# RK4 stage: VectorE writes the linear values to PSUM, the cubic weights move ahead in its order, fp32 fillers on TensorE

## The chip, the cores and the metric

The kernel runs on one core of one Trainium2 chip. The metric is the device time of the launch in microseconds (us); less is better. Three runs of the kernel before gave a median of 904.41 us.

## The reference

Four residual stages follow each other on x of shape 64 x 32 x 256: a conditioned transformer block, a GRU over time, an attention over blocks, and last the stage of this change, an RK4 integration over the 32 time steps. Cut to that stage:

```python
def _derivative(q, p, drive, coupling, bias):
    i_couple = jnp.tanh(q) @ coupling.T
    dq = q - q ** 3 / 3.0 - p + drive + i_couple + bias
    dp = EPSILON * (q + ALPHA - BETA * p)
    return (dq, dp)
# per time step: four evaluations, each from the result of the one before
dq1, dp1 = _derivative(q, p, ...)
dq2, dp2 = _derivative(q + 0.5 * DT * dq1, p + 0.5 * DT * dp1, ...)
dq3, dp3 = _derivative(q + 0.5 * DT * dq2, p + 0.5 * DT * dp2, ...)
dq4, dp4 = _derivative(q + DT * dq3, p + DT * dp3, ...)
q, p = clip(q + DT / 6 * (dq1 + 2 dq2 + 2 dq3 + dq4)), clip(p + ...)
...
x = x + q_trace      # q of every time step
```

## The kernel before, in words

The state q of a time step is kept as 128 features x 2 chunks x 64 batch entries in fp32. Each chunk ("a" and "b") is a tile of 128 x 64. The four evaluations of a step form one serial ring through three engines:

- ScalarE (ACT) takes the tanh of q by chunks (`th1a`, `th1b` to `th4b`, L1150), and the square of the whole of q (`sq1` to `sq4`, L1153), which it writes to PSUM. It also makes `V3`, `V4`, `V5` as multiples of the clipped state P (L1127) and the drives D of a later step (L1123).
- TensorE (PE; its weight loads are PEld) adds up evaluation k in a pair of PSUM banks, one for each output chunk: first `linear(k, Z)`, two products of the 128 x 128 identity with a linear value (L783), then `coupled`, four products of the coupling matrix with the tanh. The first coupled product of an output chunk streams its 64 columns twice (128 columns, L779), the last streams 64 (L778). Each fp32 matmul stands in the trace as two records. In evaluations 1 and 3 (`chunks_together`) both output chunks take tanh a first and then tanh b; in 2 and 4 (`chunks_in_turn`) the first output chunk is finished before the second is begun.
- VectorE (DVE) computes the next q from the sum in PSUM and a weight w: q2a and q2b (L1693, L1694), q3a and q3b (L1707, L1708), q4a and q4b (L1720, L1721), and qa and qb of the next step (L1736, L1737). The weight is the cubic part, made from the square and q: w1 (L1690), w2 (L1704), w3 (L1717), w4 (L1729). The linear values are E1 (L1733) for evaluation 1 and Z2, Z3, Z4 (L1685, L1702, L1713) for the others. U2, t3, s1 to s4 and P (L1683 to L1727) are parts of these and of the sum for p; L1678 clips q.
- GpSimd (POOL) adds q to the output row and makes U3, U4, m and b4.

The order of the work on each engine is the order in the code, and the tuples `RK_ACT`, `RK_DVE` and `RK_POOL` list it, because each instruction raises its engine's semaphore by one and others wait for the count. DVE's list of a step ends with q4b, s4, P, w4, E1, qa, qb. ScalarE's loop body of a step begins with V5 (made from the P of the step before), then th1a, th1b, sq1, V4; and the body before ends with th4a, th4b, sq4 and V3, which waits for P. Thus V3 and V5 stand ahead of th1a in ScalarE's queue. `mine(...)` is DVE's wait for its own earlier instruction, `coupling(k, c)` its wait for the sum of output chunk c, `act_done` its wait for ScalarE.

Of the kernel before, what the change touches and what calls it, by code (L numbers as in the profile page):

```python
# [8 lines left out]
ALU = mybir.AluOpType  # L9
AX = mybir.AxisListType  # L10

P = 128
B, T, D = 64, 32, 256
KC = D // P
# [13 lines left out]
DT, EPSILON, ALPHA, BETA, CLAMP = 0.01, 0.08, 0.7, 0.8, 20.0  # L28
# [5 lines left out]
C_ = DT / 2  # L34
A_ = EPSILON * C_
SHIFT = ALPHA / BETA
# [15 lines left out]
for _name, _n in (("ada_b", 12), ("qkv_b", 48), ("out_b", 2), ("ffn_b1", 8), ("ffn_b2", 2), ("b_ih", 6),  # L52
# [19 lines left out]
GI_STEPS = (4, 9, 13, 18, 22, 27, 31, 36)  # L72
RK_ACT = ("V5", "th1a", "th1b", "sq1", "V4", "th2a", "th2b", "sq2", "th3a", "th3b", "sq3", "Da", "Db", "th4a", "th4b",
          "sq4", "V3")
RK_DVE = ("q", "U2", "Z2", "w1", "q2a", "q2b",
          "t3", "s1", "Z3", "w2", "q3a", "q3b",
          "s2", "Z4", "s3", "w3", "q4a", "q4b",
          "s4", "P", "w4", "E1", "qa", "qb")
RK_POOL = ("store", "U4", "m", "b4", "U3")
POOL_DVE = ("score_vec", "wo_sum", "wqr", "wo_mean", "wo_c", "copy7", "scaled06", "resid06", "score06", "max06", "scaled7", "resid7", "score7",  # L80
            "score_max", "score_sub",
# [10 lines left out]
def at(step, events, name):  # L92

    return step * len(events) + events.index(name) + 1
# [7 lines left out]
def build(nc, xT, cond, ada_w, qkv_w, out_w, ffn_w1, ffn_w2, w_ih, w_hh, wk, wo, coup, vecs, out):  # L102
# [20 lines left out]
    with ctx:  # L123
# [60 lines left out]
        rk = {}  # L184
# [174 lines left out]
        def _(pe):  # L359
# [247 lines left out]
            def keep_warm(n, bank=TB):  # L607

                for _ in range(n):
                    pe.matmul(ps[:, bank, 0:P], idle[:, :], idle[:, :], start=True, stop=True)  # L610
# [160 lines left out]
            def twice(ap):  # L771

                return ap.unsqueeze(1).to_broadcast([P, 2, B])

            def coupled(k, c, kk, first, last):
                th, w = rk[f"th{k % 2}"][:, kk, :], cpc[:, kk, c * P:c * P + P]
                if last:
                    return pe.matmul(ps[:, RK_BANK[k % 2][c], 0:B], w, th, start=first, stop=last)  # L778
                return pe.matmul(ps[:, RK_BANK[k % 2][c], 0:2 * B], w, twice(th), start=first, stop=last)  # L779

            def linear(k, z):
                for c in range(KC):
                    pe.matmul(ps[:, RK_BANK[k % 2][c], 0:2 * B], ident[:, :], twice(rk[z][:, c, :]), start=True, stop=False)  # L783

            def tanh_done(t, k, half):
                pe.wait_ge(rk_act, RK_ACT_START + at(t, RK_ACT, f"th{k}{half}"))

            def chunks_in_turn(t, k):
                tanh_done(t, k, "a")
                coupled(k, 0, 0, False, False)  # L790
                tanh_done(t, k, "b")
                coupled(k, 0, 1, False, True).then_inc(rk_pe, 1)
                coupled(k, 1, 0, False, False)
                coupled(k, 1, 1, False, True).then_inc(rk_pe, 1)

            def chunks_together(t, k):
                tanh_done(t, k, "a")
                coupled(k, 0, 0, False, False)
                coupled(k, 1, 0, False, False)
                tanh_done(t, k, "b")  # L800
                coupled(k, 0, 1, False, True).then_inc(rk_pe, 1)
                coupled(k, 1, 1, False, True).then_inc(rk_pe, 1)

            keys7_mm()
            blocks_out(0, 0)
# [16 lines left out]
            def first_evaluation():  # L822
                pe.wait_ge(rk_dve, RK_START)
                for c in range(KC):
                    pe.matmul(ps[:, RK_BANK[1][c], 0:B], ident[:, :], rk["E1"][:, c, :], start=False, stop=True).then_inc(rk_pe, 1)

            for t in range(T):
                if t:
                    pe.wait_ge(rk_dve, RK_START + at(t - 1, RK_DVE, "E1"))
                    linear(1, "E1")  # L830
                    chunks_together(t, 1)
                else:
                    first_evaluation()
                pe.wait_ge(rk_dve, RK_START + at(t, RK_DVE, "Z2"))
                linear(2, "Z2")
                if t == 0:
                    keep_warm(WARM_START)
                chunks_in_turn(t, 2)
                pe.wait_ge(rk_dve, RK_START + at(t, RK_DVE, "Z3"))
                linear(3, "Z3")  # L840
                chunks_together(t, 3)
                pe.wait_ge(rk_dve, RK_START + at(t, RK_DVE, "Z4"))
                linear(4, "Z4")
                chunks_in_turn(t, 4)


        @block.scalar
# [331 lines left out]
        def _(dve):  # L1179
# [473 lines left out]
            dve.wait_ge(rk_dve, RK_START - 1)  # L1653
            dve.wait_ge(rk_act, 2)
            dve.tensor_tensor(r_["E1"], r_["D0"], r_["P"], Su).then_inc(rk_dve, 1)
            for t in range(T):
                def mine(name, step=t):
                    dve.wait_ge(rk_dve, RK_START + at(step, RK_DVE, name))

                def pool(name, step=t):  # L1660
                    dve.wait_ge(rk_pool, rk_pool_count(step, name))

                def act_done(name):
                    dve.wait_ge(rk_act, RK_ACT_START + at(t, RK_ACT, name))

                def coupling(k, c):
                    dve.wait_ge(rk_pe, 8 * t + 2 * (k - 1) + c + 1)
                    return ps[:, RK_BANK[k % 2][c], 0:B]

                def half(name, c):  # L1670
                    return rk[name][:, c, :]

                def inc(r):
                    r.then_inc(rk_dve, 1)

                if t:
                    mine("qb", t - 1)
                    inc(dve.tensor_scalar(r_["q"], r_["qraw"], CLAMP, -CLAMP, ALU.min, ALU.max))  # L1678
                else:
                    inc(dve.tensor_copy(r_["q"], r_["qraw"]))  # L1680
                if t == 0:
                    dve.wait_ge(p_dev, 5)
                inc(STT(r_["U2"], r_["P"], -K2, r_[f"D{t % 3}"], M, Ad))  # L1683
                mine("U2")
                inc(STT(r_["Z2"], r_["q"], 1 - A_ * C_, r_["U2"], M, Ad))  # L1685
                if t:
                    act_done("sq1")
                else:
                    dve.wait_ge(rk_first, 1 + RK_FIRST.index("sq1"))
                inc(STT(r_["w"], r_["qsq" if t else "w4"], -(C_ + 1), r_["q"], Ad, M))  # L1690
                a1 = coupling(1, 0)
                mine("w1")
                inc(dve.tensor_tensor(half("q2", 0), a1, half("w", 0), Su))  # L1693
                inc(dve.tensor_tensor(half("q2", 1), coupling(1, 1), half("w", 1), Su))  # L1694

                pool("U3", t - 1)
                inc(STT(r_["t3"], r_["q"], 0.5, r_["U3"], M, Ad))
                if t == 0:
                    dve.wait_ge(rk_first, 1 + RK_FIRST.index("V5"))
                inc(STT(r_["s1"], r_["q"], W1, r_["V5"], M, Ad))  # L1700
                mine("t3")
                inc(STT(r_["Z3"], r_["q2"], -A_ * C_, r_["t3"], M, Ad))  # L1702
                act_done("sq2")
                inc(STT(r_["w"], r_["qsq"], -C_, r_["q2"], Ad, M))  # L1704
                a2 = coupling(2, 0)
                mine("w2")
                inc(dve.tensor_tensor(half("q3", 0), a2, half("w", 0), Su))  # L1707
                inc(dve.tensor_tensor(half("q3", 1), coupling(2, 1), half("w", 1), Su))  # L1708

                pool("b4")  # L1710
                inc(STT(r_["s2"], r_["q2"], W2, r_["s1"], M, Ad))
                mine("q3b")
                inc(STT(r_["Z4"], r_["q3"], 2 * (1 - A_ * C_), r_["b4"], M, Ad))  # L1713
                mine("s2")
                inc(STT(r_["s3"], r_["q3"], W3, r_["s2"], M, Ad))
                act_done("sq3")
                inc(STT(r_["w"], r_["qsq"], -2 * C_, r_["q3"], Ad, M))  # L1717
                a3 = coupling(3, 0)
                mine("w3")
                inc(STT(half("q4", 0), a3, 2.0, half("w", 0), M, Su))  # L1720
                inc(STT(half("q4", 1), coupling(3, 1), 2.0, half("w", 1), M, Su))  # L1721

                mine("q4b")
                if t < T - 1:
                    inc(STT(r_["s4"], r_["q4"], W4, r_["s3"], M, Ad))
                    mine("s4")
                    inc(dve.tensor_scalar(r_["P"], r_["s4"], C_ * (CLAMP - SHIFT), C_ * (-CLAMP - SHIFT), ALU.min, ALU.max))  # L1727
                act_done("sq4")
                inc(STT(r_["w4"], r_["qsq"], -(C_ + 1) / 3, r_["q4"], Ad, M))  # L1729
                if t == T - 1:  # L1730
                    break
                mine("P")
                inc(dve.tensor_tensor(r_["E1"], r_[f"D{(t + 1) % 3}"], r_["P"], Su))  # L1733
                a4 = coupling(4, 0)
                mine("w4")
                inc(STT(half("qraw", 0), a4, 1 / 3, half("w4", 0), M, Su))  # L1736
                inc(STT(half("qraw", 1), coupling(4, 1), 1 / 3, half("w4", 1), M, Su))  # L1737

            ended = RK_START + at(T - 1, RK_DVE, "q4b")
# [322 lines left out]
```

## Time and profile before

| | |
|---|---|
| median of 3 runs | 904.41 us (902.95 to 905.20) |
| profiled execution | 902.81 us, span 900.8 us |
| TensorE, weight loads | 99%, 85% of the span |
| DVE, ACT, POOL | 66%, 46%, 33% |
| mean granted clock of TensorE | 0.998 of full speed |

The span runs from the first to the last instruction of the profiled execution. Timelines give start and duration in us, then engine, line, operation, output and inputs; equal instructions that follow each other are merged with their count. A bracket at the end is the engine's idle time before it and what released it.

### The profile page before, as it was taken

The numbers are of one execution on the slowest core, as the hardware profiler recorded it, in microseconds if no ns is written. First come the engines' busy times: TensorE is split into PE (matmuls) and PEld (weight loads), VectorE is DVE, ScalarE is ACT, GpSimd is POOL, SyncE is SP. The second block draws the span as 40 slices with busy tenths as digits, with TensorE's granted clock in tenths as the row PEclk, the third lists the DMA queues.
The fourth block names the chain that finished last, engine by engine and source line by source line (L and its number), as shares of the span: only waits on it lengthen the run. The fifth ranks groups of instructions, "written<-read, shape, count | busy, mean of one in ns | idle before, by whom it ended". The sixth has DMA issues, their size and how long they took to land.

```text
span 900.8 us, 18502 instructions
## 1 busy us (share of the span) xinstructions
PE 888.2 (99%) x7178; PEld 766.0 (85%) x7178; DVE 597.7 (66%) x1700; ACT 411.4 (46%) x1145; POOL 298.5 (33%) x383
## 2 busy tenths in 40 slices
PE   7999999999999999999999999999999899999998
PEld 6788888888888888888888878999987599999998
DVE  5644555655556545655576775777777888888887
ACT  2233332333223432234355664555545766666665
POOL 2755510102101201023623516333123555554343
PEclk9999999999999999999999999999999999999999
DMA  7222100000000000110004000000000000000000
GB/s 273 64 90 71 47 1 1 1 1 1 2 1 2 1 1 2 48 47 2 1 12 188 0 1 1 1 2 1 1 1 1 1 2 25 2 24 1 25 1 25
DMA packets 5705, 22.00 MB, mean 24 GB/s; under 512 B 881, under 2 KB 1265, under 8 KB 5233
## 3 DMA queue, kind: packets, MB, share of 16 engines
q1 hardware_dynamic: 5616, 20.82, 6.7%
q8 instruction: 56, 0.92, 0.4%
q14 instruction: 33, 0.26, 0.1%
HBM read 18.72 MB, written 2.10 MB: 23 GB/s over the span
## 4 chain that ended last, share of the span: by engine, by line
PE 93%; DVE 4%; ACT 1%; issue 1%; POOL 0%; DVEq 0%; ACTq 0%
PE ps L368 48%; PE ps L779 8%; PE ps L783 7%; PE ps L639 6%; PE ps L461 6%; PE ps L778 5%; PE ps L629 3%; PE ps L641 3%; PE ps L450 2%; PE ps L375 1%; PE ps L491 0%; DVE yt L1632 0%; DVE frs L1263 0%; PE ps L658 0%; DVE BD L1249 0%
## 5 line engine op out<-in xcount | busy, mean ns | idle before, releaser
L1208 DVE TENSOR_SCALAR qk<-ps,vec 128x512 f32<-128x512 f32 x64 | 48.0, 749 | 98.0 <-PE ps L368 97.9
L368 PE MATMUL ps<-x_hi,W_hi 128*128 128x512 f32 x256 | 102.0, 398 | 1.9 <-DVE x_lo L1331 1.6
L872 ACT ACTIVATE qk<-ps,vec 128x512 f32<-128x512 f32 x64 | 44.2, 690 | 124.8 <-PE ps L368 124.8
L368 PE MATMUL ps<-x_lo,W_hi 128*128 128x512 f32 x256 | 99.9, 390 | 0.0
L368 PE MATMUL ps<-x_hi,W_lo 128*128 128x512 f32 x256 | 99.8, 390 | 0.0
L779 PE MATMUL ps<-rk_th,cpc 128*128 128x128 f32 x516 | 98.9, 294 | 0.4 <-ACT rk_th L1150 0.2
L1219 DVE SCALAR_TENSOR_TENSOR o_lo<-ps,vec,o_hi 128x512 fp32r<-128x512 f32 x64 | 47.1, 744 | 71.7 <-ACT o_hi L888 68.2
L888 ACT ACTIVATE o_hi<-ps,vec 128x512 fp32r<-128x512 f32 x64 | 44.0, 687 | 108.3 <-PE ps L461 108.3
L779 PEld LDWEIGHTS ps<-rk_th,cpc 128*128 128x128 f32 x516 | 72.7, 191 | 9.3 <-ACT rk_th L1150 6.4
L778 PE MATMUL ps<-rk_th,cpc 128*128 128x64 f32 x508 | 77.7, 255 | 0.0
L639 PE MATMUL ps<-ht,hh 128*128 128x128 f32 x512 | 77.1, 283 | 0.4 <-DVE ht L1543 0.2
L639 PEld LDWEIGHTS ps<-ht,hh 128*128 128x128 f32 x512 | 66.0, 191 | 7.7 <-DVE ht L1543 5.3
L778 PEld LDWEIGHTS ps<-rk_th,cpc 128*128 128x128 f32 x508 | 72.1, 192 | 0.0
L1150 ACT ACTIVATE rk_th<-rk_q 128x64 f32<-128x64 f32 x192 | 44.3, 253 | 50.3 <-DVE rk_q L1707 20.2
L461 PEld LDWEIGHTS ps<-BD,V 128*128 128x128 f32 x512 | 62.1, 191 | 3.3 <-issue 1.0
L783 PE MATMUL ps<-rk_Z,ident 128*128 128x128 f32 x384 | 63.7, 288 | 0.6 <-DVE rk_Z L1685 0.6
L461 PE MATMUL ps<-BD,V 128*128 128x128 f32 x512 | 62.2, 275 | 0.0
L368 PEld LDWEIGHTS ps<-x_hi,W_hi 128*128 128x128 f32 x256 | 48.0, 188 | 13.4 <-DVE x_lo L1331 2.0
L368 PEld LDWEIGHTS ps<-x_lo,W_hi 128*128 128x128 f32 x256 | 48.0, 188 | 10.3
L368 PEld LDWEIGHTS ps<-x_hi,W_lo 128*128 128x128 f32 x256 | 48.1, 188 | 9.3
L368 PE MATMUL ps<-W_hi,x_hi 128*128 128x512 f32 x128 | 51.7, 404 | 0.0
L783 PEld LDWEIGHTS ps<-rk_Z,ident 128*128 128x128 f32 x384 | 50.6, 192 | 0.7 <-DVE rk_Z L1685 0.7
(293 smaller groups left out, 2144.2 us busy)
## 6 DMA issues: line engine op xcount, KB each, us to landing
stage<-qkv_w SPq DMA_DIRECT2D x6, 768.0 KB, 4.4
stage<-out_w SPq DMA_DIRECT2D x4, 512.0 KB, 3.8
f_raw<-ffn_w SPq DMA_DIRECT2D x2, 1024.0 KB, 4.9
xorig<-xT SPq DMA_DIRECT2D x1, 2048.0 KB, 8.7
x_all<-xT SPq DMA_DIRECT2D x1, 1536.0 KB, 14.1
out<-xtb SPq DMA_DIRECT2D x3, 512.0 KB, 3.1
ada_sb<-ada_w SPq DMA_DIRECT2D x1, 1024.0 KB, 9.7
BD<-qkv_w SPq DMA_DIRECT2D x1, 768.0 KB, 6.2
```

Source lines behind the costliest of these rows:

```text
L368: r = pe.matmul(out_, lhsT, rhs, start=first and i == 0, stop=last and i == n - 1)
L461: r = pe.matmul(ps[:, OB[h % 2], i * P:i * P + P], V[:, i, h * DH:h * DH + DH], BD[:, i * HU + h, :], start=True, stop=True)
L629: r = pe.matmul(ps[:, PJ[n % 2], :], (ih_hi if term != 1 else ih_lo)[:, c, ms], (y_hi if term != 2 else y_lo)[:, c, js], start=i % 6 == 0, ...
L639: return pe.matmul(ps[:, bank[c], 0:2 * B], hh[:, k, ms], h_.unsqueeze(1).to_broadcast([P, 2, B]), start=k == 0, stop=k == KC - 1)
L778: return pe.matmul(ps[:, RK_BANK[k % 2][c], 0:B], w, th, start=first, stop=last)
L779: return pe.matmul(ps[:, RK_BANK[k % 2][c], 0:2 * B], w, twice(th), start=first, stop=last)
L783: pe.matmul(ps[:, RK_BANK[k % 2][c], 0:2 * B], ident[:, :], twice(rk[z][:, c, :]), start=True, stop=False)
L872: act.activation(qk[:, 0, h % 2, :], ps[:, PJ[0], :], ACT.Identity, bias=col("qkv_b", HU * u + h)).then_inc(act_evac, 1)
L888: act.activation(o_hi[:, h % 2, :], ps[:, OB[h % 2], :], ACT.Identity, bias=col("qkv_b", 2 * HEADS + HU * u + h)).then_inc(ohi_done, 1)
L1150: act.activation(rk[f"th{k % 2}"][:, c, :], rk[src][:, c, :], ACT.Tanh).then_inc(rk_act, 1)
L1208: dve.tensor_scalar(qk[:, 1, h % 2, :], ps[:, PJ[1], :], col("qkv_b", HEADS + HU * u + h), None, ALU.add).then_inc(dve_evac, 1)
L1219: dve.scalar_tensor_tensor(o_lo[:, h % 2, :], ps[:, OB[h % 2], :], col("qkv_b", 2 * HEADS + HU * u + h), o_hi[:, h % 2, :].bitcast(F32), A ...
```

## The change

TensorE's identity products go, but for the one of evaluation 2 in the first time step and those of the first evaluation. In their place DVE writes the linear value itself into columns 0 to 63 of the evaluation's two PSUM banks (`seed(k)`), and the coupled products add onto it. TensorE therefore waits for the linear value and then for tanh a ahead of the same coupled product. In DVE's order w1 goes ahead of Z2, w2 ahead of Z3, w4 ahead of P, and qa ahead of E1. After each evaluation TensorE has fillers whose result nobody reads: the identity times 192 columns of the coupling matrix, and in evaluations 1 and 3 another of 128 columns, written to the unused bank TB. The orders of ACT and POOL stay.

```diff
-RK_DVE = ("q", "U2", "Z2", "w1", "q2a", "q2b",
-          "t3", "s1", "Z3", "w2", "q3a", "q3b",
+RK_DVE = ("q", "U2", "w1", "Z2", "q2a", "q2b",
+          "t3", "s1", "w2", "Z3", "q3a", "q3b",
           "s2", "Z4", "s3", "w3", "q4a", "q4b",
-          "s4", "P", "w4", "E1", "qa", "qb")
+          "s4", "w4", "P", "qa", "E1", "qb")
...
+            def fill(columns):
+                pe.matmul(ps[:, TB, 0:columns], ident[:, :], cpc[:, 0, 0:columns], start=True, stop=True)
...
             def chunks_in_turn(t, k):
...
                 coupled(k, 1, 1, False, True).then_inc(rk_pe, 1)
+                fill(192)
 
             def chunks_together(t, k):
...
                 coupled(k, 1, 1, False, True).then_inc(rk_pe, 1)
+                fill(192)
+                fill(P)
...
                     pe.wait_ge(rk_dve, RK_START + at(t - 1, RK_DVE, "E1"))
-                    linear(1, "E1")
                     chunks_together(t, 1)
...
                 pe.wait_ge(rk_dve, RK_START + at(t, RK_DVE, "Z2"))
-                linear(2, "Z2")
                 if t == 0:
+                    linear(2, "Z2")
                     keep_warm(WARM_START)
                 chunks_in_turn(t, 2)
                 pe.wait_ge(rk_dve, RK_START + at(t, RK_DVE, "Z3"))
-                linear(3, "Z3")
                 chunks_together(t, 3)
                 pe.wait_ge(rk_dve, RK_START + at(t, RK_DVE, "Z4"))
-                linear(4, "Z4")
                 chunks_in_turn(t, 4)
...
+            def seed(k):
+                lo = RK_BANK[k % 2][0]
+                return ps[:, lo:lo + KC, 0:B]
...
-                mine("U2")
-                inc(STT(r_["Z2"], r_["q"], 1 - A_ * C_, r_["U2"], M, Ad))
                 if t:
                     act_done("sq1")
                 else:
                     dve.wait_ge(rk_first, 1 + RK_FIRST.index("sq1"))
+                mine("q")
                 inc(STT(r_["w"], r_["qsq" if t else "w4"], -(C_ + 1), r_["q"], Ad, M))
+                mine("U2")
+                inc(STT(seed(2) if t else r_["Z2"], r_["q"], 1 - A_ * C_, r_["U2"], M, Ad))
...
+                act_done("sq2")
+                mine("q2b")
+                inc(STT(r_["w"], r_["qsq"], -C_, r_["q2"], Ad, M))
                 mine("t3")
-                inc(STT(r_["Z3"], r_["q2"], -A_ * C_, r_["t3"], M, Ad))
-                act_done("sq2")
-                inc(STT(r_["w"], r_["qsq"], -C_, r_["q2"], Ad, M))
+                inc(STT(seed(3), r_["q2"], -A_ * C_, r_["t3"], M, Ad))
...
-                inc(STT(r_["Z4"], r_["q3"], 2 * (1 - A_ * C_), r_["b4"], M, Ad))
+                inc(STT(seed(4), r_["q3"], 2 * (1 - A_ * C_), r_["b4"], M, Ad))
...
                     inc(STT(r_["s4"], r_["q4"], W4, r_["s3"], M, Ad))
-                    mine("s4")
-                    inc(dve.tensor_scalar(r_["P"], r_["s4"], C_ * (CLAMP - SHIFT), C_ * (-CLAMP - SHIFT), ALU.min, ALU.max))
                 act_done("sq4")
                 inc(STT(r_["w4"], r_["qsq"], -(C_ + 1) / 3, r_["q4"], Ad, M))
                 if t == T - 1:
                     break
-                mine("P")
-                inc(dve.tensor_tensor(r_["E1"], r_[f"D{(t + 1) % 3}"], r_["P"], Su))
+                mine("s4")
+                inc(dve.tensor_scalar(r_["P"], r_["s4"], C_ * (CLAMP - SHIFT), C_ * (-CLAMP - SHIFT), ALU.min, ALU.max))
                 a4 = coupling(4, 0)
                 mine("w4")
                 inc(STT(half("qraw", 0), a4, 1 / 3, half("w4", 0), M, Su))
+                mine("P")
+                inc(dve.tensor_tensor(seed(1), r_[f"D{(t + 1) % 3}"], r_["P"], Su))
                 inc(STT(half("qraw", 1), coupling(4, 1), 1 / 3, half("w4", 1), M, Su))
```

## Rows read from the trace of the kernel before

**Rows 1.** The page: busy time by engine, and the chain that ended last, by engine
```profile
...
PE 888.2 (99%) x7178; PEld 766.0 (85%) x7178; DVE 597.7 (66%) x1700; ACT 411.4 (46%) x1145; POOL 298.5 (33%) x383
...
PE 93%; DVE 4%; ACT 1%; issue 1%; POOL 0%; DVEq 0%; ACTq 0%
```

**Rows 2.** Windows: busy us (records) of PE, PEld, DVE, ACT, POOL; granted clock, DMA
```profile
...
760.00:780.00 20.00, 20.00 (x166) 19.07 (x165) 17.45 (x83) 13.65 (x61) 11.10 (x20) 1.00 0.02 6
14.30:17.60 3.30, 3.30 (x17) 3.30 (x17) 3.30 (x3) 0.00 (x0) 1.08 (x1) 0.50 1.02 425
```

**Rows 3.** One line's instructions: count, ns (min/median/max), first and last start
```profile
L1736 DVE SCALAR_TENSOR_TENSOR rk_qraw<-ps,rk_w x31: 212/215/219, 715.1 to 891.5; 128x64 f32<-128x64 f32 x31
```

**Rows 4.** Waits from 730 to 895 us: total us, times, longest
```profile
ACT rk_V L1127 <- DVE rk_P L1727: 6.4, 28, 0.2
```

**Rows 5.** Timeline of DVE, 762 to 768 us: start, duration
```profile
...
763.13 0.29 DVE L1685 SCALAR_TENSOR_TENSOR rk_Z<-rk_q,ps 128x128 f32<-128x128 f32 x1
763.33 0.28 DVE L1690 SCALAR_TENSOR_TENSOR rk_w<-ps,rk_q 128x128 f32<-128x128 f32 x1
763.72 0.23 DVE L1693 TENSOR_TENSOR rk_q<-ps,rk_w 128x64 f32<-128x64 f32 x1
...
764.99 0.23 DVE L1707 TENSOR_TENSOR rk_q<-ps,rk_w 128x64 f32<-128x64 f32 x1
...
766.55 0.23 DVE L1720 SCALAR_TENSOR_TENSOR rk_q<-ps,rk_w 128x64 f32<-128x64 f32 x1
766.77 0.23 DVE L1721 SCALAR_TENSOR_TENSOR rk_q<-ps,rk_w 128x64 f32<-128x64 f32 x1
767.03 0.30 DVE L1725 SCALAR_TENSOR_TENSOR ps<-rk_q,ps 128x128 f32<-128x128 f32 x1
767.36 0.29 DVE L1727 TENSOR_SCALAR rk_P<-ps 128x128 f32<-128x128 f32 x1
767.57 0.28 DVE L1729 SCALAR_TENSOR_TENSOR rk_w<-ps,rk_q 128x128 f32<-128x128 f32 x1
```

**Rows 6.** Timeline of ACT (ScalarE), 762 to 768 us
```profile
...
762.35 0.56 ACT L1150 ACTIVATE rk_th<-rk_qraw 128x64 f32<-128x64 f32 x2
...
763.98 0.40 ACT L1150 ACTIVATE rk_th<-rk_q 128x64 f32<-128x64 f32 x2 [0.55 <-DVE rk_q L1693]
...
765.24 0.26 ACT L1150 ACTIVATE rk_th<-rk_q 128x64 f32<-128x64 f32 x1 [0.69 <-DVE rk_q L1707]
...
765.85 0.26 ACT L1153 ACTIVATE ps<-rk_q 128x128 f32<-128x128 f32 x1
766.05 0.57 ACT L1123 ACTIVATE rk_D<-xtb,db 128x64 f32<-128x64 f32 x2
...
767.19 0.26 ACT L1153 ACTIVATE ps<-rk_q 128x128 f32<-128x128 f32 x1
767.68 0.31 ACT L1127 ACTIVATE rk_V<-rk_P 128x128 f32<-128x128 f32 x1 [0.23 <-DVE rk_P L1727]
767.90 0.26 ACT L1127 ACTIVATE ps<-rk_P 128x128 f32<-128x128 f32 x1
```

**Rows 7.** Timeline of TensorE's weight loads, 762 to 768 us
```profile
...
764.29 0.30 PEld L779 LDWEIGHTS ps<-rk_th,cpc 128*128 128x128 f32 x2 [0.19 <-ACT rk_th L1150]
...
765.17 0.53 PEld L783 LDWEIGHTS ps<-rk_Z,ident 128*128 128x128 f32 x4
765.62 0.53 PEld L779 LDWEIGHTS ps<-rk_th,cpc 128*128 128x128 f32 x4
```

**Rows 8.** Two lines' semaphore records: DVE's L1658, TensorE's L752
```profile
L1658 DVEq EVENT_SEMAPHORE  x127: 21/21/21, 710.5 to 895.9; - x127
...
L752 PEldq EVENT_SEMAPHORE  x1: 1905/1905/1905, 693.4 to 693.4; - x1
```

**Rows 9.** Timeline, 694.5 to 695.45 us, around the wait of L752
```profile
...
694.60 0.63 ACT L1100 ACTIVATE s_at<-s_at 128x512 f32<-128x512 f32 x1 [2.18 <-DVE s_at L1609]
...
695.30 0.30 PEld L754 LDWEIGHTS ps<-s_at,ident 128*128 128x128 f32 x2 [0.47 <-issue]
```

More of the change, by code:

```diff
@@ L777, in coupled @@
                 if last:
-                    return pe.matmul(ps[:, RK_BANK[k % 2][c], 0:B], w, th, start=first, stop=last)
-                return pe.matmul(ps[:, RK_BANK[k % 2][c], 0:2 * B], w, twice(th), start=first, stop=last)
+                    return pe.matmul(ps[:, RK_BANK[k % 2][c], 0:B], w, th, start=first, stop=last, skip_group_check=True)
+                return pe.matmul(ps[:, RK_BANK[k % 2][c], 0:2 * B], w, twice(th), start=first, stop=last, skip_group_check=True)
             def linear(k, z):
                 for c in range(KC):
-                    pe.matmul(ps[:, RK_BANK[k % 2][c], 0:2 * B], ident[:, :], twice(rk[z][:, c, :]), start=True, stop=False)
+                    pe.matmul(ps[:, RK_BANK[k % 2][c], 0:2 * B], ident[:, :], twice(rk[z][:, c, :]), start=True, stop=False, skip_group_check=True)
             def tanh_done(t, k, half):
                 pe.wait_ge(rk_act, RK_ACT_START + at(t, RK_ACT, f"th{k}{half}"))
+            def fill(columns):
+                pe.matmul(ps[:, TB, 0:columns], ident[:, :], cpc[:, 0, 0:columns], start=True, stop=True)
             def chunks_in_turn(t, k):
@@ L824, in first_evaluation @@
                 for c in range(KC):
-                    pe.matmul(ps[:, RK_BANK[1][c], 0:B], ident[:, :], rk["E1"][:, c, :], start=False, stop=True).then_inc(rk_pe, 1)
+                    pe.matmul(ps[:, RK_BANK[1][c], 0:B], ident[:, :], rk["E1"][:, c, :], start=False, stop=True, skip_group_check=True).then_inc(rk_pe, 1)
             for t in range(T):
```

## The prediction

> **What bounds the kernel now.** The page first [rows 1]: TensorE is busy 888.2 of 900.8 us and carries 93% of the chain that ended last. The reader might take it for a TensorE-bound kernel. But a matmul's recorded time includes its latency, so that share says little of small products. RK4 is the last stage; line 1736 (qa) ran 31 times from 715.1 to 891.5 us [rows 3]: 176.4 / 30 = 5.88 us a step, and I take 5.87 for an undisturbed one. The windows give 166 matmul records in 20 us, at clock 1.00 [rows 2]; that is 48 to 49 a step, two for each of 24 fp32 matmuls. Loads follow each other by 0.11 us in a dense stream (765.17 to 765.62: four) [rows 7], so the step's 48 loads need 5.4 us. TensorE is nearly full, but not the whole bound; what remains is waiting in a ring of three engines. So I read one step in time on VectorE (DVE), ScalarE and TensorE's loads [rows 5 to 7] and add from start to start. Names are those of the kernel's order lists.
>
> The ring now. All of it from [rows 5 to 7]. q2a (L1693) starts at 763.72 and q3a (L1707) at 764.99: 1.27. Tanh 2a starts at 763.98, its product's first load at 764.29, which is 0.31 later: 0.26 of tanh and 0.05 to get through. From that load to q3a 0.70. In evaluation 3 tanh starts at 765.24 but its first load at 765.62, 0.07 later than 0.31 would give, because the four identity loads begin at 765.17 only. Then 0.93 to q4a and 1.15 to q4b. q2a itself waits for the weight: w1 ran 763.33 to 763.61, after Z2 at 763.13, and q2a came 0.39 after w1's start. From q2a to q4b 763.72 to 766.77: 3.05. From q4b to the next q2a 5.87 - 3.05 = 2.82.
>
> **The change, part by part.** *Removed:* 8 identity matmuls a step, 16 records by 0.11 = 1.8 us of TensorE [rows 7]. *Added:* fillers. Two of 128 columns are 4 records by 0.11; for 192 columns there is no row. Bounds: 0.11 (the pace of the loads, as before) and 0.17 (in proportion to the columns); I take 0.17, as nothing shows that more columns are free: 8 by 0.17 = 1.36, and with 0.44 for the others 1.8 us. TensorE's load stays what it was. Do they delay the products? In evaluations 1 and 3 the last product load lies 0.14 before q2a or q4a, and the next tanh's load comes 0.57 after it: 0.71 of room against the 0.11 of the last load and 0.56 of fillers. In 2 and 4 it is at least 0.5 against 0.11 + 0.34. So I cost them at nothing; if each filler took 0.1 more, evaluations 1 and 3 would start their next product about 0.1 late, 6 us in all.
>
> *Linear values written by DVE:* Z2, Z3, Z4, E1 keep their instruction, only the target becomes PSUM. DVE's s4 at 767.03 writes PSUM in 0.30 us, w4 at 767.57 writes SBUF in 0.28 [rows 5], so at most 0.02, and that off the ring (the tanh is later); I take nothing. What it gives: the 0.07 of evaluation 3.
>
> *A second wait in front of the tanh's product.* Before, the Z wait stood ahead of the identity products and the tanh wait alone ahead of the coupled ones. Now both stand in front of one matmul. Where DVE has two waits ahead of one instruction (q2a: the product and w1) the trace has a separate 21 ns EVENT_SEMAPHORE, 127 of them at L1658 [rows 8], and q2a starts 0.11 after w1's end (763.61 to 763.72). With one wait the start comes 0.03 after: s4 ends at 767.33, P is at 767.36 [rows 5]. So 0.07 to 0.08 on DVE. TensorE has such records too; one that was waited out is L752's [rows 8]: exp ends 695.23, the load is at 695.30, 0.07 after, against 0.05 with one wait [rows 9]. Call the price e: 0.02 by that row, up to 0.08 by DVE's, and 0 if the wait that is drawn out is the one on Z, done long before. I take 0.05, between them: L752 stood behind three waits, DVE's pattern is the same two, and is seen 127 times.
>
> *w1, w2 ahead of Z2, Z3.* w1 moves up by up to 0.2, so q2a is no longer bound by it but by its product. But then w2 waits for the square, Z3 follows it by 0.20, and q3a follows Z3 by 0.20. q2b now follows q2a by a product's 0.22 (as 766.55 to 766.77), where DVE's own pace was all that parted them; from there 0.42 to the square (as q4b at 766.77 to 767.19) and 0.30 to w2 (0.26 of square, 0.04 to get through) [rows 5, 6]. q2a to q3a is thus the larger of 0.57 + e + 0.70 = 1.27 + e and 0.22 + 0.42 + 0.30 + 0.40 = 1.34. So this is no gain: 1.27 before.
>
> *w4 ahead of P: the heart of it.* w4 needs the square of q4; P needs only s4. Before, P started at 767.36 and w4 at 767.57 without waiting. The square starts 767.19, lasts 0.26, plus 0.04: w4 can't start before 767.49. P behind it starts at 767.69, 0.33 later than before. And ScalarE's order has V3 and V5, both made from P, ahead of the next tanh 1a: V3 at 767.68, V5 0.22 later; both move by 0.33. A 128-column activation gives way to the next after 0.20 (765.85 to 766.05) [rows 6]. V3 waited for P in 28 steps even before [rows 4]. Tanh 1a started 0.32 after V5 (762.35; V5 a step earlier than 767.90 is 762.03), so it had 0.12 of slack, and is now held. New tail, from q4b: 0.42 to the square (766.77 to 767.19) [rows 5, 6], 0.30 to w4, 0.20 to P, 0.32 to V3, 0.22 to V5, 0.20 to tanh 1a, 0.31 + e to the load, 0.93 to q2a (evaluation 3's 765.62 to 766.55, same order of products): 2.90 + e.
>
> **The sum.** q2a to q3a 1.34; q3a to tanh 0.25; to the load 0.31 + e; to q4b 1.15; tail 2.90 + e: 5.95 + 2e, or 5.88 + 3e where e is above 0.07. With e = 0.05: 6.05, against 5.87: +0.18. By 31 steps +5.6 us. The other stages aren't touched. *Against which time.* The profiled execution took 902.81 us (span 900.8); with the sum 908.4. The median of the runs shown, 904.41, is 1.6 above that execution, so its scale gives 910.0. Between the two I say 909.
>
> The clock, weighed by its rows: the granted clock is 1.00 (2.4 GHz) in RK4 and 0.50 (1.2 GHz) from 14.3 to 17.6 us, where 17 loads took 3.30 us, 0.19 each, against 0.11 [rows 2, 7]. The new step streams about as many columns as the old one, with pauses that I estimate from the room above at 0.1 to 0.5 us, so I leave it at 1.00.
> The Trainium skill ("TensorE: Matmul & The Clock Gate", "Part 1: The HAM clock gate") says that the clock falls to half after idleness. By that rule a step whose TensorE pauses too much would be priced as the third rival below; by the rows, at nothing.
>
> **Rivals.**
> *The second wait is free and little is lost* (e near 0, or V5 lets the tanh go after 0.16): 5.91 to 5.95, +0.04 to +0.08, by 31 = +1.2 to +2.5 us: about 906. For: L752. Against: DVE's 127 rows.
> *Faster: TensorE's stream was the bound.* If P's delay fits into the slack before tanh 1a (0.12) and the early w1 and evaluation 3 count in full: 0.12 + 0.07 + 0.03 for E1's loads = 0.22 a step, 31 times 6.8: 897.6. For: 99% busy. It decides if P starts no more than about 0.1 later; against: by the square's row it starts 0.33 later.
> *The clock falls to half* (slower too). 18 loads of the ring (4 to q3a, 8 to q4b, 6 to q2a) by 0.08 more = 1.4 a step, 31 times 45 us on top of the forecast: 954. For: only that pauses are new.
>
> **How the numbers follow.** Forecast (slower by 3 to 8 us) 0.62; within no more than 2.7 us 0.24; faster 0.11; clock 0.03. 0.3%, 2.7 us, is about what a measurement of this kernel can tell. The range: from e = 0 and the short V5, 904.4 + 1.2, less 2 for a scatter like that of the runs shown and for a part of the gains, to e = 0.08 (6.12, +7.8) 912.2: 903.5 to 913.
>
> **What would show it.** Right: P at least 0.25 later after q4b, V3 to V5 to tanh 1a without a gap, w4 idle about 0.2 for the square; the first load 0.08 to 0.13 after a tanh's end; step 6.0. Wrong: tanh 1a still waiting for qa; loads 0.05 after the tanh; fillers' matmuls ending after the next tanh; clock below 1.00.

## The result and the profile after

The kernel after took 907.83 us (median of 5 runs, 907.39 to 910.15) against 904.41 us for the kernel before (5 runs, 902.59 to 905.31). The ratio is 1.0053, interval 1.0038 to 1.0068: slower, outside the 0.3% that a measurement can tell, and inside the range of the forecast (909.0, 903.5 to 913.0). The medians differ by 3.4 us, which is 1.0038; the ratio is taken over all runs and says about 4.8 us. The two disagree because the five runs of the kernel before lie in two groups, 902.59 and 902.95, and 904.41 to 905.31, and the median fell in the upper one. In 57 later runs of it, on the three chips of the experiments below, the median is 902.60 us. The profiled span went from 900.8 to 905.7 us.

The page of the kernel after: busy time by engine, and the chain that ended last [beside rows 1].

```profile
...
PE 889.2 (98%) x7054; PEld 760.2 (84%) x7054; DVE 602.6 (67%) x1700; ACT 408.9 (45%) x1145; POOL 298.5 (33%) x383
...
PE 91%; DVE 5%; ACT 2%; issue 2%; POOL 0%; DVEq 0%; ACTq 0%
```

TensorE lost 124 records, yet its share of the span hardly moved. What moved is the chain: DVE and ACT have 7% of it instead of 5%, and "issue" 2% instead of 1%. The same 20 us as in [rows 2], as a window:

```profile
...
760.00:780.00 20.00, 19.60 (x150) 17.98 (x148) 17.32 (x81) 12.65 (x56) 10.56 (x20) 1.00 0.08 28
```

The granted clock is 1.00, and the weight loads are busy 17.98 of 20 us instead of 19.07: TensorE waits more. The length of a step is read from qa, as in [rows 3]:

```profile
L1744 DVE SCALAR_TENSOR_TENSOR rk_qraw<-ps,rk_w x31: 214/219/224, 714.6 to 896.1; 128x64 f32<-128x64 f32 x31
```

From the first qa (714.6) to the last (896.1) there are 181.5 us; 181.5 / 30 = 6.05 us against 5.88. The difference of 0.17 by 30 steps is 5.1 us, all of the 4.9 us that the span grew. An undisturbed step is 6.04 us. Now one step on DVE (timeline, beside [rows 5]):

```profile
762.03 0.23 DVE L1731 SCALAR_TENSOR_TENSOR rk_q<-ps,rk_w 128x64 f32<-128x64 f32 x1
762.29 0.30 DVE L1735 SCALAR_TENSOR_TENSOR ps<-rk_q,ps 128x128 f32<-128x128 f32 x1
762.75 0.29 DVE L1737 SCALAR_TENSOR_TENSOR rk_w<-ps,rk_q 128x128 f32<-128x128 f32 x1 [0.16 <-ACT ps L1157]
762.96 0.28 DVE L1741 TENSOR_SCALAR rk_P<-ps 128x128 f32<-128x128 f32 x1
763.16 0.22 DVE L1744 SCALAR_TENSOR_TENSOR rk_qraw<-ps,rk_w 128x64 f32<-128x64 f32 x1
763.29 0.29 DVE L1746 TENSOR_TENSOR ps<-rk_D,rk_P 128x128 f32<-128x128 f32 x1
763.60 0.23 DVE L1747 SCALAR_TENSOR_TENSOR rk_qraw<-ps,rk_w 128x64 f32<-128x64 f32 x1
763.86 0.35 DVE L1686 TENSOR_SCALAR rk_q<-rk_qraw 128x128 f32<-128x128 f32 x1
...
764.97 0.22 DVE L1702 TENSOR_TENSOR rk_q<-ps,rk_w 128x64 f32<-128x64 f32 x1
...
766.31 0.22 DVE L1717 TENSOR_TENSOR rk_q<-ps,rk_w 128x64 f32<-128x64 f32 x1
```

on ScalarE (timeline, beside [rows 6]):

```profile
762.46 0.26 ACT L1157 ACTIVATE ps<-rk_q 128x128 f32<-128x128 f32 x1
763.27 0.31 ACT L1131 ACTIVATE rk_V<-rk_P 128x128 f32<-128x128 f32 x1 [0.56 <-DVE rk_P L1741]
763.49 0.26 ACT L1131 ACTIVATE ps<-rk_P 128x128 f32<-128x128 f32 x1
763.69 0.42 ACT L1154 ACTIVATE rk_th<-rk_qraw 128x64 f32<-128x64 f32 x2
...
766.57 0.26 ACT L1154 ACTIVATE rk_th<-rk_q 128x64 f32<-128x64 f32 x1 [0.69 <-DVE rk_q L1717]
```

and on TensorE's weight loads (timeline, beside [rows 7]):

```profile
764.04 0.52 PEld L779 LDWEIGHTS ps<-rk_th,cpc 128*128 128x128 f32 x4 [0.40 <-DVE rk_qraw L1747]
...
766.93 0.41 PEld L779 LDWEIGHTS ps<-rk_th,cpc 128*128 128x128 f32 x3
```

The tail from q4b (762.03) reads: square 762.46, w4 762.75, P 762.96, V3 763.27, V5 763.49, tanh 1a 763.69, load 764.04, q2a 764.97. In steps 0.43, 0.29, 0.21, 0.31, 0.22, 0.20, 0.35, 0.93, in sum 2.94, where the forecast had 2.90 + e = 2.95. P follows q4b by 0.93 instead of 0.59 (767.36 less 766.77 in [rows 5]), so it is 0.34 late. DVE sits idle 0.16 for the square, ScalarE 0.56 for P. Nothing parts V3, V5 and tanh 1a but ScalarE's own pace: over steps 2 to 29 tanh 1a always follows V5 by 0.199 to 0.201 (0.313 to 0.318 before). qa, from which the tanh is made, started 0.53 before it. The wait of [rows 4] has grown from 6.4 us to 15.0 (view of waits, 730 to 895 us):

```profile
ACT rk_V L1131 <- DVE rk_P L1741: 15.0, 27, 0.6
```

From q2a to q3a there are 1.34 us. Tanh 3a starts at 766.57 and its load at 766.93: 0.36, so e is 0.05; the median over steps 2 to 29 is 0.370, so e is rather 0.06. TensorE shows the separate record of a second wait (its line's instructions), as DVE did in [rows 8]:

```profile
L786 PEldq EVENT_SEMAPHORE  x126: 51/51/51, 712.2 to 901.4; - x126
```

### The profile page after: what moved, and what is told of

Its sections match the earlier page's. It is cut to its first block, busy times and chain, and to the rows that moved or that the text cites. A ratio compares the mean times of both kernels' runs of the same rounds, so it can differ in the third digit from the quotient of the medians.

```text
span 905.7 us, 18444 instructions
## 1 busy us (share of the span) xinstructions
PE 889.2 (98%) x7054; PEld 760.2 (84%) x7054; DVE 602.6 (67%) x1700; ACT 408.9 (45%) x1145; POOL 298.5 (33%) x383
## 4 chain that ended last, share of the span: by engine, by line
PE 91%; DVE 5%; ACT 2%; issue 2%; POOL 0%; DVEq 0%; ACTq 0%
PE ps L368 48%; PE ps L779 8%; PE ps L639 6%; PE ps L461 6%; PE ps L789 6%; PE ps L778 5%; PE ps L629 3%; PE ps L641 3%; PE ps L450 2%; PE ps L375 1%; PE ps L491 0%; ACT rk_th L1154 0%; DVE yt L1636 0%; DVE frs L1267 0%; PE ps L658 0%
## 5 line engine op out<-in xcount | busy, mean ns | idle before, releaser
L779 PE MATMUL ps<-rk_th,cpc 128*128 128x128 f32 x516 | 101.6, 299 | 4.3 <-ACT rk_th L1154 0.2
L789 PE MATMUL ps<-cpc,ident 128*128 128x192 f32 x380 | 83.0, 327 | 0.0
L1154 ACT ACTIVATE rk_th<-rk_q 128x64 f32<-128x64 f32 x192 | 46.6, 256 | 47.8 <-DVE rk_q L1717 20.2
L789 PEld LDWEIGHTS ps<-cpc,ident 128*128 128x128 f32 x380 | 59.0, 191 | 0.0
```

Source lines behind the costliest of these rows:

```text
L789: pe.matmul(ps[:, TB, 0:columns], ident[:, :], cpc[:, 0, 0:columns], start=True, stop=True)
L1154: act.activation(rk[f"th{k % 2}"][:, c, :], rk[src][:, c, :], ACT.Tanh).then_inc(rk_act, 1)
```

## The experiments

The theory was the one of the prediction: P's delay holds tanh 1a, and the second wait costs e in each evaluation whose first load the ring waits for; fillers and PSUM targets cost nothing. The rivals were that the fillers or the new dependences of the seeds cost the time, and that TensorE's stream was the bound all along. Step times are (last less first start of qa) / 30, with an undisturbed step (the median over the steps) behind a slash; where the text gives it to three places it is from the same starts in ns. Each kernel was compared with the kernel before on the same chip (medians there 902.60, 902.54 and 903.48 us).

| kernel | us (range) | ratio (interval) | step, us |
|---|---|---|---|
| after | 907.83 (907.39 to 910.15) | 1.0053 (1.0038 to 1.0068) | 6.05 / 6.04 |
| e1_p_first | 910.59 (909.88 to 913.89) | 1.0095 (1.0078 to 1.0111) | 6.15 / 6.14 |
| e2_tanh_wait_first | 904.01 (903.80 to 906.30) | 1.0017 (1.0007 to 1.0026) | 5.93 / 5.91 |
| e3_both | 907.97 (906.50 to 909.38) | 1.0056 (1.0042 to 1.0070) | 6.03 / 6.01 |
| e4_no_fillers | 907.57 (907.43 to 948.39) | 1.0053 (1.0040 to 1.0065) | 6.05 / 6.03 |
| e5_tail_as_before | 903.65 (903.40 to 905.92) | 1.0014 (1.0005 to 1.0023) | 5.92 / 5.90 |
| e6_tail_and_wait | 901.86 (899.49 to 902.92) | 0.9983 (0.9973 to 0.9993) | 5.79 / 5.78 |
| e7_before_w4_first | 908.05 (907.96 to 910.04) | 1.0063 (1.0051 to 1.0076) | 6.06 / 6.05 |
| e8_orders_as_before | 902.32 (901.84 to 904.72) | 0.9999 (0.9989 to 1.0008) | 5.88 / 5.87 |
| e9_first_step | 899.12 (898.86 to 900.87) | 0.9955 (0.9942 to 0.9969) | 5.78 / 5.77 |
| e10_no_fillers | 899.49 (898.80 to 901.50) | 0.9961 (0.9947 to 0.9975) | 5.78 / 5.77 |
| e11_fillers_twice | 940.81 (939.34 to 942.17) | 1.0413 (1.0395 to 1.0431) | 7.07 |

**P ahead of w4 again, the rest as after (e1_p_first).**

```diff
-          "s4", "w4", "P", "qa", "E1", "qb")
+          "s4", "P", "w4", "qa", "E1", "qb")
```

> The changed kernel with P ahead of w4 again. Theory A (P's late start and the second wait on TensorE make the loss, each a part of it): P starts about 0.33 us earlier after q4b, V3 and V5 no longer hold tanh 1a, the step falls from 6.04 to 5.90 to 5.93 us, that is 3.5 to 4.5 us less than the changed kernel and 1 to 2 us more than the kernel before. Rival B (the fillers are in the way of the products): no change, 907 to 908. Rival C (the wait alone is the loss): no change either.

It missed: 6.15 instead of a gain. P is in time, but a new delay came. The timeline of the tail of e1, all engines:

```profile
873.62 0.29 DVE L1737 TENSOR_SCALAR rk_P<-ps 128x128 f32<-128x128 f32 x1
...
874.21 0.22 DVE L1744 SCALAR_TENSOR_TENSOR rk_qraw<-ps,rk_w 128x64 f32<-128x64 f32 x1
...
874.33 0.46 POOL L2031 TENSOR_TENSOR rk_U<-rk_D,rk_V 128x128 f32<-128x128 f32 x1 [2.98 <-ACT rk_V L1131]
...
874.35 0.59 DVE L1746 TENSOR_TENSOR ps<-rk_D,rk_P 128x128 f32<-128x128 f32 x1
...
874.85 0.21 DVE L1747 SCALAR_TENSOR_TENSOR rk_qraw<-ps,rk_w 128x64 f32<-128x64 f32 x1
874.99 0.41 PEld L779 LDWEIGHTS ps<-rk_th,cpc 128*128 128x128 f32 x3 [0.35 <-DVE ps L1746]
```

U3 on GpSimd waits for V3 and so for P. With the earlier P it starts at 874.33, 0.02 before E1, and E1 takes 0.59 us instead of 0.29. E1 now has to be in PSUM before TensorE's first load, and it is what that load waited for; qb behind E1 is late too. It is so in most steps (the line's instructions: min, median, max in ns, of e1 and then of e5, where E1 stands ahead of qa):

```profile
L1746 DVE TENSOR_TENSOR ps<-rk_D,rk_P x31: 292/587/594, 714.5 to 898.9; 128x128 f32<-128x128 f32 x31
```

```profile
L1743 DVE TENSOR_TENSOR ps<-rk_D,rk_P x31: 290/290/290, 714.6 to 892.1; 128x128 f32<-128x128 f32 x31
```

The Trainium skill ("SBUF — State Buffer", "SBUF: two separate sides") says that DVE and GpSimd share a pair of ports as an exclusive lock: a DVE operation with two SBUF inputs and a GpSimd operation that reads SBUF shut each other out for a whole instruction. The trace agrees: E1 reads D and P from SBUF, U3 reads D and V, and E1 ends 0.15 after U3 does.

**TensorE waits for the tanh first, then for the linear value (e2_tanh_wait_first).** Both waits still stand ahead of the same matmul.

```diff
             def chunks_in_turn(t, k):
                 tanh_done(t, k, "a")
+                linear_done(t, k)
...
-                pe.wait_ge(rk_dve, RK_START + at(t, RK_DVE, "Z3"))
                 chunks_together(t, 3)
```

> The changed kernel with TensorE's wait for tanh a issued ahead of its wait for the linear value, so that the tanh's is the one that stays on the matmul and the linear value's becomes the separate record. Theory A: the first load comes 0.05 after the tanh instead of 0.11; it counts once in evaluation 3 and once in evaluation 1, so the step falls by 0.11 to 0.12, to 5.92, about 3.5 us less than the changed kernel. Rival B and a rival D (P's delay alone is the loss): no change.

It held: 5.93 a step. In the timeline of e2 tanh 3a and its load lie 0.31 apart, as with one wait, against 0.36:

```profile
765.80 0.26 ACT L1156 ACTIVATE rk_th<-rk_q 128x64 f32<-128x64 f32 x1 [0.69 <-DVE rk_q L1719]
...
766.11 0.30 PEld L779 LDWEIGHTS ps<-rk_th,cpc 128*128 128x128 f32 x2
```

The separate record, which stood at the tanh's wait (L786) in the kernel after, now stands at the linear value's:

```profile
L792 PEldq EVENT_SEMAPHORE  x127: 51/51/51, 710.2 to 896.8; - x127
```

There are as many waits as before. So the price e belongs to the order in which the waits are given, not to their number: it is paid where the wait given last is also the one that ends last.

**Both edits together (e3_both).** No further diff.

> Both edits together. Theory A: step 5.79 to 5.82, so 1.5 to 2.5 us below the kernel before (ratio about 0.998). If the two parts share one slack, the step stays near 5.90 and the time at or above that of before.

It missed for the reason of e1: E1 beside U3. The swapped waits gave 0.13 here too (6.14 to 6.01), but not in evaluation 1. There the late E1 is now the wait given last, and the first load comes 0.586 after tanh 1a instead of 0.524 in e1 (medians over steps 2 to 29), one e later. Evaluations 2 and 3 gave one e each (0.370 to 0.307).

**The kernel after without fillers (e4_no_fillers).**

```diff
                 coupled(k, 1, 1, False, True).then_inc(rk_pe, 1)
-                fill(192)
...
-                fill(192)
-                fill(P)
```

> The changed kernel without any filler. Theory A: the fillers lie in pauses and cost nothing, so at an unchanged clock the step stays at 6.03 to 6.04 and the time within 1 us of the changed kernel's. Rival B: the step falls by 0.1 or more. If instead the granted clock falls to 0.5 in parts of this stage, the time rises by as much as 45 us.

The step is the same, 6.05, so the fillers cost nothing. In the window the loads have 109 records instead of 148 and the clock stays at 1.00:

```profile
...
760.00:780.00 20.00, 14.41 (x108) 13.03 (x109) 17.34 (x81) 12.48 (x57) 10.56 (x20) 1.00 0.07 27
```

One of its five runs took 948.39 us at a mean clock of 0.912. The ratio leaves that run out; what came of it stands with e10.

**DVE's tail as before, the rest as after (e5_tail_as_before).** Both P and E1 go back to their places, so that E1 runs before U3.

```diff
-          "s4", "w4", "P", "qa", "E1", "qb")
+          "s4", "P", "w4", "E1", "qa", "qb")
```

> The changed kernel with DVE's tail in the order of before, s4, P, w4, E1, qa, qb (E1 still written to PSUM). E1 has two SBUF inputs; in e1_p_first it ran beside GpSimd's U3 and took 0.59 us instead of 0.29, and qb behind it came 0.3 late. Theory A with this collision added: here E1 is over before U3 starts, the tail is as before, and the step falls from 6.04 to 5.88 to 5.92 us, that is 3.5 to 5 us under the changed kernel, ratio to the kernel before 1.001 to 1.002. Rival E (P ahead of w4 is itself what slows e1_p_first): the step stays at 6.1 or more.

5.92, so the tail's order costs 6.037 - 5.900 = 0.137 a step, 4.2 us over 31. E1 takes 0.29 each time (above). This run undoes two moves at once, P's and E1's; P's alone was e1.

**The tail as before and the tanh's wait first (e6_tail_and_wait).** e5's and e2's edits.

> The same, and TensorE's wait for tanh a ahead of its wait for the linear value. Theory A: both parts count in full, step 5.77 to 5.80, 2 to 3 us below the kernel before, ratio 0.997 to 0.998. If the products' or DVE's own chain sets a floor near the step of before, the ratio stays at 1.000.

5.79, and for the first time less than before. The timeline of e6's tail on ScalarE:

```profile
769.72 0.26 ACT L1159 ACTIVATE ps<-rk_q 128x128 f32<-128x128 f32 x1
770.20 0.31 ACT L1133 ACTIVATE rk_V<-rk_P 128x128 f32<-128x128 f32 x1 [0.22 <-DVE rk_P L1739]
770.42 0.26 ACT L1133 ACTIVATE ps<-rk_P 128x128 f32<-128x128 f32 x1
770.73 0.64 ACT L1156 ACTIVATE rk_th<-rk_qraw 128x64 f32<-128x64 f32 x2
```

Between V5 and the tanh there are 0.31 us again instead of 0.20: the tanh waits for qa, not for V5.

**The kernel before with w4 ahead of P, and nothing else (e7_before_w4_first).**

```diff
-          "s4", "P", "w4", "E1", "qa", "qb")
+          "s4", "w4", "P", "E1", "qa", "qb")
```

> The kernel before with one edit: w4 ahead of P (identity products, order of w1, w2, E1 and waits as before). Theory A: P starts 0.33 later after q4b, tanh 1a and 1b about 0.2 later, of which the slack before the next q2a takes 0.12: step 5.94 to 5.98, 2.5 to 3.5 us more than before, ratio 1.003 to 1.004. Rival F (P's delay costs only in the changed kernel, where nothing else fills TensorE): ratio 1.000.

The direction held, the size did not: 6.06 instead of 5.94 to 5.98, so that this one swap costs as much as the whole change. Its timeline on DVE:

```profile
762.88 0.29 DVE L1727 SCALAR_TENSOR_TENSOR rk_w<-ps,rk_q 128x128 f32<-128x128 f32 x1 [0.16 <-ACT ps L1153]
763.09 0.28 DVE L1731 TENSOR_SCALAR rk_P<-ps 128x128 f32<-128x128 f32 x1
763.40 0.29 DVE L1733 TENSOR_TENSOR rk_E<-rk_D,rk_P 128x128 f32<-128x128 f32 x1
763.62 0.22 DVE L1736 SCALAR_TENSOR_TENSOR rk_qraw<-ps,rk_w 128x64 f32<-128x64 f32 x1
```

E1 waits for the late P, and qa stands behind E1: qa comes 0.74 after w4's start here, 0.41 in the kernel after. So the last link differs. On ScalarE (timeline of e7):

```profile
763.62 0.26 ACT L1127 ACTIVATE ps<-rk_P 128x128 f32<-128x128 f32 x1
763.87 0.40 ACT L1150 ACTIVATE rk_th<-rk_qraw 128x64 f32<-128x64 f32 x2
```

The tanh starts 0.25 after V5 and 0.25 after qa (763.62), the distance from qa that it had in the kernel before. Here it is held by P, E1 and qa; V5 would have let it go about 0.05 earlier, at its pace of 0.20. e7 thus shows what a late P costs, and the path over V3 and V5 is shown by the rows of the kernel after. The expectation put tanh 1a 0.2 later after q4b and gave 0.12 of that to slack; by the medians it came 0.255 later and q2b 0.221 later (3.175 against 2.954), so that the slack was 0.03.

**Seeds, fillers and swapped waits, all of DVE's orders as before (e8_orders_as_before).**

```diff
+RK_DVE = ("q", "U2", "Z2", "w1", "q2a", "q2b",
+          "t3", "s1", "Z3", "w2", "q3a", "q3b",
           "s2", "Z4", "s3", "w3", "q4a", "q4b",
           "s4", "P", "w4", "E1", "qa", "qb")
```

> Linear values in PSUM, fillers, tanh's wait first, and the whole of DVE's order as before, so that only the identity products' going is left of the change. Theory A: q2a is held by w1 behind Z2 as before, tanh 3's load comes 0.07 earlier but q4a is held by w3: step 5.85 to 5.87, ratio 0.999 to 1.000. If the identity products had bound the step: 5.75 or less, ratio 0.996.

5.88, ratio 0.9999: taking the identity products off TensorE, with fillers in their place, gives nothing in this order of DVE. What e6 has beyond e8 is w1 and w2 ahead, 0.09 a step. On DVE in e8 (timeline) w1 stands behind Z2, which itself follows U2 by 0.33:

```profile
768.34 0.29 DVE L1693 SCALAR_TENSOR_TENSOR ps<-rk_P,rk_D 128x128 f32<-128x128 f32 x1
768.67 0.29 DVE L1695 SCALAR_TENSOR_TENSOR ps<-rk_q,ps 128x128 f32<-128x128 f32 x1
768.88 0.28 DVE L1700 SCALAR_TENSOR_TENSOR rk_w<-ps,rk_q 128x128 f32<-128x128 f32 x1
769.26 0.23 DVE L1703 TENSOR_TENSOR rk_q<-ps,rk_w 128x64 f32<-128x64 f32 x1
```

Tanh 1a starts at 767.81 in that step, so q2a comes 1.45 after it; in e6 that is 764.96 to 766.32, 1.36.

**e6 with Z2 ahead of w1 in the first time step alone (e9_first_step).** In e6 the first step looks long (6.51 us from its q2a to the next, against 6.21 before): w1 stands there ahead of Z2, for which TensorE's last identity products wait.

```diff
                 inc(STT(seed(2) if t else r_["Z2"], r_["q"], 1 - A_ * C_, r_["U2"], M, Ad))
+                if t == 0:
+                    dve.wait_ge(rk_first, 1 + RK_FIRST.index("sq1"))
+                    inc(STT(r_["w"], r_["w4"], -(C_ + 1), r_["q"], Ad, M))
```

> e6_tail_and_wait with Z2 ahead of w1 in the first time step alone. There TensorE still has the identity products of Z2 and the twelve warming matmuls behind Z2, and with w1 first the first step took 6.5 us from q2a to q2a, against 6.2 with the order of before. Theory A: the first step is back at about 6.2, so 0.3 us less than e6; ratio to the kernel before 0.997 to 0.998.

899.12 us, ratio 0.9955 (0.9942 to 0.9969): it beats both kernels. From q2a to q2a the first step takes 6.13. But most of the 2.7 us between the medians of e6 and e9 did not come from there, and the reason given for the edit does not hold. Counted from DVE's copy of q that opens the stage to the first qa, it is 708.82 to 714.93 in e9 and 711.97 to 718.15 in e6: 6.11 against 6.18. In e6 only q2a came early; the product behind it did not. The stage began 3.15 us later in e6's profiled execution. Far ahead of it the granted clock was 0.50 in both, for 6.8 us, but in e9 about 5 us earlier (windows of e6, and then two of e9):

```profile
...
20.60:27.30 6.70, 5.61 (x13) 4.45 (x14) 3.35 (x12) 2.60 (x3) 4.66 (x4) 0.50 0.14 29
```

```profile
...
20.60:27.30 6.70, 6.52 (x31) 5.28 (x29) 4.99 (x13) 3.29 (x4) 4.78 (x4) 0.85 0.19 37
...
15.80:22.60 6.80, 6.62 (x39) 6.16 (x38) 6.57 (x11) 2.27 (x3) 0.16 (x1) 0.50 0.41 167
```

Two of e6's eleven runs took 899.49 and 899.73 us, at mean granted clocks of 1.00 and 0.998; the others took 901.70 to 902.92, at 0.994 to 0.996. What lengthened their start is open. The stage itself, from that copy to the end of the span, is 191.9 us before (900.8 less 708.93), 189.2 in e6 and 188.7 in e9. That gain, 2.7 and 3.2 us, is what the edits are worth; the 4.4 us between the medians of e9 and of the kernel before also holds differences ahead of the stage.

**e9 without fillers (e10_no_fillers).**

> The same without fillers. Theory A (fillers only hold the clock): at an unchanged clock the step stays at 5.77 to 5.78 us and the time within 0.5 us of e9; but as one run of e4_no_fillers took 948 us with a mean clock of 0.912, at least one of the runs here should show a clock below 0.98 and 20 us or more on top. Rival G (that run was an accident unrelated to fillers): all runs near 901.

The step and the time are those of e9. The run with a low clock that was expected did not come. Its window has 112 records and clock 1.00, and its six runs had mean clocks of 0.994 to 1.00:

```profile
...
760.00:780.00 20.00, 15.47 (x112) 13.55 (x112) 17.15 (x84) 13.35 (x60) 11.41 (x21) 1.00 0.00 0
```

**The kernel after with every filler twice (e11_fillers_twice).**

```diff
                 fill(192)
+                fill(192)
...
                 fill(P)
+                fill(192)
+                fill(P)
```

> The changed kernel with every filler twice. The after trace leaves about 0.1 us between the end of the fillers of evaluations 1, 2 and 3 and the next product's matmul. Theory A: added fillers of 0.60 (evaluations 1, 3) and 0.38 us (2, 4) overrun this room by 0.5 and 0.26, so evaluation 1 and 2 alone add 0.75 a step and evaluation 3 up to 0.5 more: step 6.8 to 7.3, time 930 to 945. Rival H (a filler that isn't needed yields or runs beside the products): time stays within 2 us of 908.

7.07 a step. The loads are busy 20.00 of 20.00 us, so this kernel is bound by TensorE's stream, while the kernel after (17.98) is not:

```profile
...
760.00:780.00 20.00, 20.00 (x160) 20.00 (x160) 15.45 (x69) 11.15 (x49) 9.66 (x18) 1.00 0.07 28
```

## Why the prediction was right, step by step

**The heart, P behind w4: right, and shown.** Alone in the kernel before (e7) it costs 0.19 a step, there through E1 and qa; taken back out of the kernel after together with E1's place (e5) it gives back 0.137. That the tanh is held over V3 and V5 in the kernel after is read from its rows, in every step from 2 to 29. The tail was forecast at 2.95 and measured 2.94. Taken back alone (e1) it did not pay, for another reason than the prediction named; the two-part undoing of e5 was needed to see its price.

**The second wait: right in place and size.** e was taken as 0.05 and is 0.06. Swapping the two waits removes it: 6.037 to 5.908 (e2), and 5.900 to 5.775 (e6), 0.13 and 0.125 a step, two times e. From the kernel after to e2 q2b comes 0.064 earlier after q4b, and q4b 0.063 earlier after q3a: evaluations 1 and 3, as forecast. The working left open that e might be nil if the wait drawn out is the one on Z. With the tanh's wait given first that is what e2 does. The records show which is drawn out: the wait given last, at L786 (tanh) in the kernel after and at L792 (linear value) in e2.

**The two losses add up.** Four kernels have them both, one or none: the tail costs 0.137 with the slow wait (after against e5) and 0.133 without it (e2 against e6), the wait 0.129 with the new tail and 0.125 with the old. So neither hides the other. The way from the kernel before to the kernel after can be gone in four steps: seeds and fillers with the free wait 0.00 (e8), w1 and w2 ahead -0.09 (e6), the second wait +0.125 (e5), the tail +0.137. Their sum is +0.17 by construction; what the runs add is the size of each.

**Fillers at nothing, TensorE not the bound: right, and shown** by e4 and e10, where taking them out changes no step, and by e11, which shows how a step looks that the stream does bind. One sign that the prediction named as speaking against it did show: a filler record ends after the next tanh. These four end at 765.76 by the profile, and tanh 2a runs from 765.22 to 765.48 (timeline of TensorE in the kernel after):

```profile
764.99 0.77 PE L789 MATMUL ps<-cpc,ident 128*128 128x192 f32 x4
```

It delays nothing, as e4 shows; by the loads, the last filler (765.37) gives way to the tanh's first (765.59).

**PSUM targets at nothing: right for the instruction, incomplete for its dependence.** E1 takes 287 to 292 ns into PSUM, against 280 to 283 into SBUF before, and off the ring in the kernel after. But the prediction had no term for what runs beside it. In the kernel after, the clip of q at 763.86 runs beside U3 (763.67, 0.45 us) and takes 0.35 us instead of the 0.23 that it took at 762.66 in the kernel before. By the rows it costs nothing, as q2a is held by its product there; no run tested it alone. In e1 and e3 the same meeting falls on E1 and decides the time.

**"So this is no gain" for w1 and w2 ahead: right for this kernel, not for every order of the tail.** The path over q2b, square, w2 and Z3 gave the 1.34 as forecast. It has that length only because q2b follows q2a by 0.22 at the product's pace. In e6, with the tail restored, w1 holds q2a again, q2b follows 0.14 later, and the early w1 is worth 0.09 a step.

**Evaluation 3's 0.07: a gain at q4b, and none in the old order.** The prediction counted it in full. e8 has the seeds, the free wait and the old orders, and its step is 5.867 against 5.863. The traces show where the 0.07 goes (medians over steps 2 to 29): tanh 3a to its load is 0.307 instead of 0.379, but q3a to q4a is 1.571 and 1.570, because q4a comes 0.39 after w3's start in both. Only q4b is 0.07 earlier, and from q4a to the next q2a it is 3.03 both times. So in the old order that gain stopped at DVE's weights. In the kernel after, where the tail is counted from q4b, q3a to q4b is 1.766 instead of 1.787: about the 0.07 less one e, as in the sum.

**The sum:** 6.04 against 6.05, +0.17 a step against +0.18. Counted from DVE's copy of q that opens the stage to the end of the span, the stage took 197.3 us (905.7 less 708.39) against 191.9: +5.4 where +5.6 was forecast. In the profiled execution it also began 0.5 us earlier, so that the span grew by 4.9. By terms (medians over steps 2 to 29): q2a to q3a 1.34 against 1.34 forecast, q3a to q4b 1.77 against 1.76, q4b to q2a 2.93 against 2.95. The forecast of 909 is 1.2 above the median. It was scaled half way up to 904.41, which the 57 later runs of the kernel before (median 902.60) show to be high; from the profiled execution alone the sum gave 908.4, and the profiled execution of the kernel after took 907.53.

**Rivals.** That the second wait is free is false as the change was made and true once the waits are swapped. That rival's 5.91 also needs the short V5, which did not come: with that alone the sum gives 6.01. That TensorE's stream was the bound is refuted by e4 for the kernel after, and by e9 and e10 for the order with the old tail: 5.78 a step with fillers and without. e8 alone would not settle it, as its fillers stayed; no run has DVE's old order with neither identity products nor fillers. That the clock falls to half did not come in the kernel after. Whether the fillers guard against it is open: without them one run of five (e4) fell to a mean clock of 0.912 and took 948.39 us, but none of six of e10, which leaves TensorE as idle, and none with fillers. One such run settles nothing.

## What to carry to other kernels

When an instruction is moved ahead of another, price the one that is passed: here P lost 0.34 us, and through ScalarE's fixed order V3 and V5 took the loss to the tanh that the whole ring waits for, while w4, which was moved up, started only 0.08 earlier after q4b (0.716 against 0.798, medians). Where two waits stand ahead of one TensorE instruction, try giving the one that comes last in time first: it was worth one e at each such place here. Before a value's target is changed so that the next engine has to wait for it, look at what runs on GpSimd beside it: an operation on DVE that nobody waited for at 0.29 us became the one that everyone waited for at 0.59.

## What the runs showed of the hardware that was not expected

- The order of two waits ahead of one TensorE instruction is worth 0.06 us each time: 0.370 against 0.307 us from a tanh's start to its load (medians, after and e2). It is 0.13 us a step, by 31 steps 4.0 us; the ratio goes from 1.0053 to 1.0017.
- A DVE tensor-tensor of 128x128 fp32 with two SBUF inputs and a PSUM output takes 0.29 us alone and 0.59 beside a GpSimd tensor-tensor; DVE's clip from SBUF to SBUF, with one such input, 0.23 and 0.35. qa in e1 and qb in the kernel after, which read PSUM and one SBUF tile, stayed at 0.22 and 0.23 beside the same U3.
- TensorE with 108 and 112 matmul records in 20 us (e4, e10), a third fewer than the 166 of before, kept a granted clock of 1.00 in that window.
